# Weighing the values in three fp16 passes, with a second exp for the high halves

## What is computed

```python
h = einsum('bhid,oi,od->bho', x, weighted_sum, weight)          # x: 8, 512, 256, 4
h = h + attention(layernorm(h))                                 # 16 heads of 16, rope, q and k normed
#   scores = einsum('bhqd,bhkd->bhqk', q, k) * SCALE
#   attn = softmax(scores);  out = einsum('bhqk,bhkd->bhqd', attn, v);  out @ out_w.T + out_b
h = h + experts(layernorm(h))                                   # 8 experts, 256 -> 1024 -> 256, gated
```

## Time and profile before

| what | before |
|---|---|
| median of three runs | 2021.08 us |
| the profiled execution | 2029.17 us |
| its span, first to last instruction | 2027.4 us |
| TensorE (PE) busy | 1911.6 us, 94% |
| ScalarE (ACT) busy | 1142.6 us, 56% |
| VectorE (DVE) busy | 792.3 us, 39% |
| GpSimd (POOL) busy | 678.6 us, 33% |
| exps (line 636) | 512 of 512 columns, 262.3 + 18.0 us |
| weighing matmuls (line 788) | 1024 records, 137.2 us |

### The profile page before, as it was taken

The page is one execution under the profiler, slowest core; times in us unless marked ns, Lnnn a source line. Parts: engine busy times, 40 slices in busy tenths (PEclk is TensorE's granted clock), DMA queues, the critical chain, the costliest instruction groups (busy, mean ns, idle before and its releaser), DMA issues.

```text
span 2027.4 us, 36619 instructions
## 1 busy us (share of the span) xinstructions
PE 1911.6 (94%) x13152; PEld 1211.9 (60%) x13152; DVE 792.3 (39%) x1660; ACT 1142.6 (56%) x1969; POOL 678.6 (33%) x570
## 2 busy tenths in 40 slices
PE   5679888899999999999999999999999999999999
PEld 4246543577547764567646675467655776456666
DVE  6756933547203380145602472133810456013000
ACT  2644666544765457644765447654576446754444
POOL 1103422324323242333423343232423334233443
PEclk8779999999999999999999999999999999999999
DMA  4113332332112221131212312122221322113221
GB/s 154 38 53 113 105 130 84 123 138 84 63 64 105 97 83 63 66 130 67 84 63 87 113 66 81 63 105 95 72 75 63 109 91 84 63 63 103 104 96 53
DMA packets 40461, 176.92 MB, mean 87 GB/s; under 512 B 4056, under 2 KB 17120, under 8 KB 23904
## 3 DMA queue, kind: packets, MB, share of 16 engines
q1 hardware_dynamic: 40288, 174.52, 24.2%
HBM read 153.54 MB, written 20.97 MB: 86 GB/s over the span
## 4 chain that ended last, share of the span: by engine, by line
PE 77%; issue 7%; DVE 7%; ACT 2%; POOL 1%; ACTq 0%; DVEq 0%; POOLq 0%
PE bank_h L859 28%; PE bank_f L878 10%; PE bank_f L880 10%; PE bank_f L881 10%; PE bank_o L788 5%; PE bank_s L776 3%; PE bank_s L692 2%; PE bank_s L693 2%; PE bank_s L694 2%; DVE tmp_b L976 1%; PE bank_s L761 1%; POOL hl L549 1%; DVE y L899 1%; PE bank_s L842 1%; ACT hh L669 1%
## 5 line engine op out<-in xcount | busy, mean ns | idle before, releaser
L549 POOL TENSOR_TENSOR hl<-h,hh 128x512 f16<-128x512 f32 x512 | 608.4, 1189 | 1148.2 <-ACT hh L669 670.7
L859 PE MATMUL bank_h<-x,w1s 128*128 128x512 f16 x3072 | 756.0, 383 | 19.5 <-issue 9.1
L666 ACT ACTIVATE h<-bank_h,b1s 128x512 f32<-128x512 f32 x512 | 353.5, 690 | 468.6 <-PE bank_h L859 452.7
L878 PE MATMUL bank_f<-w2s,hh 128*128 128x256 f16 x2048 | 563.2, 275 | 2.1 <-DVE acc L1091 1.3
L880 PE MATMUL bank_f<-w2s,hh 128*128 128x256 f16 x2048 | 561.1, 274 | 0.0
L881 PE MATMUL bank_f<-w2s,hl 128*128 128x256 f16 x2048 | 560.9, 274 | 0.0
L859 PEld LDWEIGHTS bank_h<-x,w1s 128*128 128x128 f16 x3072 | 287.6, 99 | 345.7 <-issue 49.9
L669 ACT ACTIVATE hh<-bank_h,b1s 128x512 f16<-128x512 f32 x512 | 352.7, 689 | 0.0
L636 ACT ACTIVATE probs<-bank_s 128x512 f32<-128x512 f32 x480 | 262.3, 604 | 153.7 <-PE bank_s L776 153.6
L878 PEld LDWEIGHTS bank_f<-w2s,hh 128*128 128x128 f16 x2048 | 202.2, 99 | 113.8 <-issue 41.0
L1091 DVE SCALAR_TENSOR_TENSOR acc<-bank_f,gw,acc 128x256 f32<-128x256 f32 x256 | 106.1, 476 | 349.9 <-PE bank_f L881 349.8
(11 more groups left out here) (137 smaller groups left out, 1788.8 us busy)
## 6 DMA issues: line engine op xcount, KB each, us to landing
w1s<-w_parts SPq DMA_DIRECT2D x56, 1024.0 KB, 4.8
w2s<-w_parts SPq DMA_DIRECT2D x56, 1024.0 KB, 4.8
xraw<-in_x_t_dram SPq DMA_DIRECT2D x32, 512.0 KB, 4.1
raw<-in_w_dram SPq DMA_DIRECT2D x16, 1024.0 KB, 6.4
w_parts<-w1s SPq DMA_DIRECT2D x8, 1024.0 KB, 8.8
w_parts<-w2s SPq DMA_DIRECT2D x8, 1024.0 KB, 10.7
out_dram<-acc SPq DMA_DIRECT2D x16, 256.0 KB, 6.1
raw<-in_qkv_w_t_dram SPq DMA_DIRECT2D x1, 768.0 KB, 6.8
```

The lines of the kernel that those rows point to most:

```text
L549: pool.tensor_tensor(hl[n % HBUFS][:], h32[n % 2][:], hh[n % HBUFS][:], ALU.subtract)\
L666: act.activation(h32[n % 2][:], bank_h[n % 2][:, :], ACT.Relu, bias=b1s[:, e, m:m + 1]).then_inc(h_hi.sem, 1)
L859: last = pe.matmul(bank_h[n % 2][:, :], w[:, wp, k, m * P:(m + 1) * P], x16[:, xp, k, :], start=(k == 0 and wp + xp == 0), stop=(k == DK - ...
L878: pe.matmul(o, high, w[:, 0, m, :], start=(m == 0 and t % 2 == 0), stop=False, skip_group_check=True)
```

## The change

From the second batch on, the values are weighed in fp16 halves:

- The scores of two heads lie in one pair of banks (`both_s`, `both_h`), and an exp reads both at once: 1024 columns. ScalarE makes it twice, once in fp32 into `exps` (which is the memory of `qk`), once straight into fp16, the high halves. TensorE waits for both exps before it writes the next scores.
- A new VectorE step, `halves`, takes the difference of the two as the low halves, 1024 columns, 32 times a batch. It has a place of its own in the list, 0.8 of a step after its `scores`.
- `weigh` is three passes of four fp16 matmuls, in place of four fp32 matmuls. It waits for `halves`.
- The values are cut in two by VectorE: a sum into `tmp_b`, a copy to fp16, a difference, where there was one sum.
- Two exps of 512 columns for a step in the first batch stay, with the fp32 weighing; its values lie in the memory of `w2s[1]`.
- So that the values fit fp16, `projections` now begins with `scale_values`: VectorE takes a maximum over the value weights, GpSimd the maximum over the partitions, VectorE makes a power of two from it in a chain of small steps and scales the weights and the bias of the values and the output weights. ScalarE waits for that before it copies the weights.

```diff
@@ attention_order
-        steps.append((first + PACE * n, "scores", n))
+        steps += [(first + PACE * n, "scores", n), (first + PACE * (n + 0.8), "halves", n)]
@@ ScalarE, scores
+                    wait(act, scored, ab, 2 * n + 2)
+                    wait(act, qk_unit, ab, TT)
+                    wait(act, halved, ab - 1, n - 1)
+                    act.activation(exps[n % 2], score_banks(n, fb is None)[:, :, :], ACT.Exp, scale=SCORE_SCALE)\
+                       .then_inc(exped.sem, 1)
                     if half == 0:
                         wait(act, weighed, ab, u - 1)
-                    for j in range(2):
-                        wait(act, scored, ab, 2 * n + j + 1)
-                        act.activation(probs[u % 2][:, 2 * half + j, :], score_bank(2 * n + j, fb is None)[:, :], ACT.Exp,
-                                       scale=SCORE_SCALE).then_inc(exped.sem, 1)
+                    act.activation(halves[u % 2][:, 0, 2 * half:2 * half + 2, :], score_banks(n, fb is None)[:, :, :],
+                                   ACT.Exp, scale=SCORE_SCALE).then_inc(exped.sem, 1)
@@ TensorE, scores and weigh
+                    if not first_batch(fb):
+                        wait(pe, exped, ab, 2 * n)
...
+                        wait(pe, halved, ab - 1, 2 * (n + 1))
...
+                    for vp, pp in ((0, 0), (1, 0), (0, 1)):
+                        for j in range(4):
+                            h = 4 * g + j
+                            last = pe.matmul(bank_o[32 * j:32 * j + 32, :],
+                                             v1[:, vp, tile, h, :, :].rearrange("p s d -> p (s d)"),
+                                             halves[n % 2][:, pp, j, :], start=(tile == 0 and vp + pp == 0),
+                                             stop=(tile == TT - 1 and pp == 1), skip_group_check=True)
@@ VectorE, qkv and halves
+                    values = tmp_b[:, 0:D]
+                    wait(dve, summed, ab, n)
+                    half_v.link(dve, dve.tensor_tensor(values, at_v[:, 0:D], qkvb[:, 2 * D:QKV], ALU.add))
+                    values = values.rearrange("p (h d) -> p h d", d=HD)
+                    half_v.link(dve, dve.tensor_copy(v1[:, 0, n, :, 0, :], values))
+                    dve.tensor_tensor(v1[:, 1, n, :, 0, :], values, v1[:, 0, n, :, 0, :], ALU.subtract)\
                        .then_inc(qkv_out.sem, 1)
...
+                elif stage == "halves":
+                    u, half = divmod(n, 2)
+                    high, low = (halves[u % 2][:, part, 2 * half:2 * half + 2, :] for part in range(2))
+                    wait(dve, exped, ab, 2 * n + 2)
+                    dve.tensor_tensor(low, exps[n % 2], high, ALU.subtract).then_inc(halved.sem, 1)
@@ projections
-                    act.wait_ge(proj_in, 32)
+                    act.wait_ge(v_scaled, 1)
+                elif stage == "projections":
+                    pool.wait_ge(v_max, 1)
+                    pool.partition_all_reduce(vmxr[:], vmx[:], P, bass.bass_isa.ReduceOp.max).then_inc(v_max_all, 1)
+            def scale_values():
+                dve.wait_ge(proj_in, 32)
+                dve.tensor_reduce(vmx[:], w_v, AX.X, ALU.max, apply_absolute_value=True).then_inc(v_max, 1)
...
+                dve.wait_ge(v_max_all, 1)
...
+                dve.tensor_scalar(w_v, w_v, vscl[:, 0:1], None, ALU.mult)
+                dve.tensor_scalar(raw_out, raw_out, vscl[:, 1:2], None, ALU.mult)
+                dve.tensor_scalar(b_v, b_v, vscl[:, 0:1], None, ALU.mult).then_inc(v_scaled, 1)
```

More of the change, by code:

```diff
@@ L143, in bodies @@
     first = [("mix_weights", 0)]
-    for step in attention_order(alone=True):
+    for step in [s for s in attention_order(alone=True) if s[1] != "halves"]:
         first += [step[1:]] + between.get(step[1:], [])
@@ L208, in bank, with two_banks @@
             return ctx.enter_context(nc.psum_tensor(name, [P, 512], F32))
+        def two_banks(name):
+            return ctx.enter_context(nc.psum_tensor(name, [P, 2, 512], F32))
         def sem(name):
@@ L251, in build @@
         kt = sb("kt", [P, HEADS // 2, TOKENS], F16)
-        v1 = sb("v1", [P, TT, HEADS, 2, HD])
+        v1 = sb("v1", [P, 2, TT, HEADS, 2, HD], F16)
+        v_first = w2s[1][:].rearrange("p s k d -> p (s k d)").bitcast(F32)\
+            .rearrange("p (t h s d) -> p t h s d", t=TT, h=HEADS, s=2)
         probs = [sb(f"probs{i}", [P, 4, TOKENS]) for i in range(2)]
+        halves = [p[:].rearrange("p j t -> p (j t)").bitcast(F16).rearrange("p (s j t) -> p s j t", s=2, j=4)
+                  for p in probs]
+        exps = [qk[:, 2 * i:2 * i + 2, :] for i in range(2)]
         xh = sb("xh", [P, XK, P], F32R)
@@ L292, in build @@
         scl = sb("scl", [P, 2])
-        bank_s = [bank(f"bank_s{i}") for i in range(2)]
+        vmx = sb("vmx", [P, DK])
+        vmxr = sb("vmxr", [P, DK])
+        vbound = sb("vbound", [P, 2])
+        vscl = sb("vscl", [P, 2])
+        both_s = two_banks("bank_s")
+        bank_s = [both_s[:, i, :] for i in range(2)]
         bank_m = bank("bank_m")
         bank_o = bank("bank_o")
-        bank_h = [bank(f"bank_h{i}") for i in range(2)]
+        both_h = two_banks("bank_h")
+        bank_h = [both_h[:, i, :] for i in range(2)]
         bank_f = [bank(f"bank_f{i}") for i in range(2)]
@@ L308, in build @@
         mix_made = [sem(f"mix_made{i}") for i in range(2)]
+        v_max = sem("v_max")
+        v_max_all = sem("v_max_all")
+        v_scaled = sem("v_scaled")
         set_hi = sem("set_hi")
@@ L379, in build, with score_banks, first_batch @@
         block = ctx.enter_context(nc.Block())
-        def score_bank(n, alone):
-            return ([bank_s[0], bank_s[1], bank_h[0], bank_h[1]] if alone else bank_s)[n % (4 if alone else 2)]
+        def score_banks(n, alone):
+            return both_h if alone and n % 2 else both_s
+        def first_batch(fb):
+            return fb is None
         def qkv_banks(t, alone):
@@ L673, in steps @@
                     act.wait_ge(scales, e + 1)
+                    if e == 1 and p == PIECES // 2:
+                        wait(act, weighed, 0, UNITS)
                     if e >= 2 and p == 0:
@@ L779, in steps @@
                     g, tile = divmod(n, TT)
-                    wait(pe, exped, ab, 4 * (n + 1))
+                    if first_batch(fb):
+                        wait(pe, exped, ab, 4 * (n + 1))
+                    else:
+                        wait(pe, halved, ab - 1, 2 * (n + 1))
                     if n == 0:
@@ L785, in steps @@
                         wait(pe, o_out, ab, g)
-                    for j in range(4):
-                        h = 4 * g + j
-                        last = pe.matmul(bank_o[32 * j:32 * j + 32, :],
-                                         v1[:, tile, h, :, :].rearrange("p s d -> p (s d)"),
-                                         probs[n % 2][:, j, :], start=(tile == 0), stop=(tile == TT - 1),
-                                         skip_group_check=True)
+                    if first_batch(fb):
+                        for j in range(4):
+                            last = pe.matmul(bank_o[32 * j:32 * j + 32, :],
+                                             v_first[:, tile, 4 * g + j, :, :].rearrange("p s d -> p (s d)"),
+                                             probs[n % 2][:, j, :], start=(tile == 0), stop=(tile == TT - 1),
+                                             skip_group_check=True)
+                        last.then_inc(weighed.sem, 1)
+                        return
+                    for vp, pp in ((0, 0), (1, 0), (0, 1)):
+                        for j in range(4):
+                            h = 4 * g + j
+                            last = pe.matmul(bank_o[32 * j:32 * j + 32, :],
+                                             v1[:, vp, tile, h, :, :].rearrange("p s d -> p (s d)"),
+                                             halves[n % 2][:, pp, j, :], start=(tile == 0 and vp + pp == 0),
+                                             stop=(tile == TT - 1 and pp == 1), skip_group_check=True)
                     last.then_inc(weighed.sem, 1)
@@ L917, in steps @@
                         att_v.start(ab)
+                        if not first_batch(fb):
+                            half_v.start(ab - 1)
                     wait(dve, x_in[n % 2], ab, 16 * (n // 2 + 1))
```

45 lines of the change are left out of this document (39 added, 6 removed).

## The result

The changed kernel takes 2168.14 us (median of four, 2166.88 to 2169.57), against 2024.07 for the kernel before, run beside it (four, 2020.14 to 2027.73): 1.071 times as long, 95% interval 1.069 to 1.073. The forecast was 2120, with 2060 to 2190 as its range. The profiled executions stand 137.7 us apart in their spans (2027.4 and 2165.1), where the sum had 99.

A forecast was written before the change was run, and what follows sets the result against it. TensorE alone was taken to set the pace in the score steps. Merged batches 72, second batch 18, values' steps 1 and start 8 made +99 us on 2029.2, or 2128; from the median 2021, 2120. Range 2060 to 2190.

The forecast's parts named there:

- The exp: ScalarE's exp of 1024 columns: 0.90 us from one to the next, two holding ScalarE 1.80 in place of 0.98.
- The weighing: Three fp16 passes on TensorE: 0.80 us in place of 1.00, bounds 0.77 and 0.96; 0.6 gained a round.
- The walk of a round: Six score steps: TensorE waits 1.49, 0.68 and 0.41 us for exps; 18.14 in place of 16.16.
- The front of a batch: Values' two more VectorE steps ahead of the rotation, about 0.4 us each: 1 us for all 28 tiles, bounds 0 and 25.
- The second batch: Score steps beside the experts' preparation, with ScalarE late: +18 us, bounds 6 and 26; VectorE's halves put at 0.
- The start: Scaling delays ScalarE's weight copies, v_scaled at 24.5 us: +8, bounds 4 and 11; extra memsets fall into GpSimd's waiting.
- TensorE wasn't the bound: Rival, chance 0.07: TensorE stays the bound in the score steps, a round is 15.56 us, 2007 in all.
- ScalarE wasn't full either: Rival, chance 0.09: ScalarE is the bound with hand-overs hidden, 15.8 us a round, 2023 in all.
- the three passes do run side by side: Rival, chance 0.03, claimed they don't: a weighing takes 2.76 us, a round 21.4, 2227 in all.
- the rival on the clock: Chance 0.10: after TensorE's waits in the rounds the clock falls to 1.2 GHz, 67 us on top, 2187.

## Why the prediction was right, and by how much it was short

The direction and the mechanism were right, and the time lies in the range, 48 us above the number. 39 of these are missing in the sum, by the two profiled executions; the rest is the spread of the kernel before (2020 to 2028), from whose low end the forecast started. Step by step:

- **The exp**: 0.90 from one to the next and 1.04 long, as taken from the copy of 1024 columns. The Trainium skill (ScalarE: Activation LUTs, Rules for kernel authors) has about 0.3 us and 0.83 ns an element for an instruction with its bias as a pointer operand. The estimate of 1.15 from it doesn't apply here, since the exps have no such operand, and the rows of this case held.
- **The weighing**: 0.77, where 0.80 was taken; that is the low bound, so nothing of the dozen weight loads shows.
- **The walk of a round**: waits of 1.49, 0.68 and 0.41 were predicted, 1.40 to 1.66, 0.74 and 0.41 measured, at the very scores named, and 94.3 us for the steps (18.25 a round) where 18.14 a round and 94 were forecast. The run without the large fp32 exp shows that the second exp is the cause, the one with the old order that the order is worth 2.7 us of the 12, and those with high halves from VectorE (81.0) and of high exps alone (76.3) that nothing else in the change holds the steps up by more than the 1.2 us of waits for VectorE in the former.
- **The front of a batch** was mis-sized: 1 us was taken for the values' steps in all, and batch 3 shows 2.0 a batch. The run with one step gives back 0.9 of it; the other 1.1 stays open, though the two waits of which the 2.0 are made do go with the values' steps. The cast among them takes 1.26 us, where about 0.4 was taken: see below. With it, a batch costs 13.4 in place of 12.2, +7 over six.
- **The second batch**: 15.5 where 18 was taken, 14.0 of them in its score steps (120.0 us against 106.0). The prediction named ScalarE as the cause and put VectorE at 0. TensorE's waits there are 16.5 us for ScalarE and 18.2 us for VectorE's low halves, since VectorE also cuts the experts' weights, so 0 isn't shown to hold. But these 18.2 us aren't VectorE's price either: before, TensorE waited 13.3 us for exps in the same steps. With the small fp32 exp the weighing still waits 15.1 us for VectorE, and the steps take 104.7 us, less than before:

```profile
PE bank_o L843 <- DVE probs L1077: 15.1, 7, 4.0
```

  That points to the second exp for most of the 14.0. As that kernel also shortens VectorE's step, no run parts the two. That VectorE can hold up this batch the kernel with its extra copies shows (118.8 us for the steps, with no second exp at all).
- **The start**: 9.6 where 8 was taken. The maximum over the partitions began 5.70 us after GpSimd had got free, near the 5.98 of the earlier trace rows, and took 0.37; but GpSimd had got free 1.6 later than the forecast had it. The two extra memsets aren't the reason: they lie in its waiting, as forecast, of which 1.71 us are left, and the cast is released by the landing of `b2sb` at 16.6 us. It lands at 15.6 to 16.8 us in all other kernels, those with the memsets of before included; the trace of the kernel before, with 14.73, was the early one. ScalarE began its copies at 25.38 against 16.47. In the changed kernel:

```profile
16.60 0.29 POOL L603 CAST ident<-ident 128x128 f16<-128x128 f32 x1 [1.71 <-DMA b2sb<-in_b_dram]
...
22.59 0.37 POOL L585 PARTITION_ALL_REDUCE vmxr<-vmx  x1 [5.70 <-issue]
...
25.38 1.48 ACT L609 ACTIVATE qkvw<-raw 128x1536 fp32r<-128x1536 f32 x1 [7.96 <-DVE qkvb L1209]
```

- **What was missing**: the stop at the loop top and the lower clock behind it, 6 to 8 us in each of five batches, 32 us of the 39 that the sum is short. No term of the prediction asked where the code of TensorE comes to lie. That it counts is shown both ways: the kernel before gets the stop by 128 instructions more ahead of the loop, and the changed one loses it by another 128. That gives back 30 of the 32 us; the stops alone are 24.4.
- **The rivals**: TensorE wasn't the bound, ScalarE wasn't full either, the clock stayed at its upper level in the steps, and the three passes do run side by side. The clock did fall elsewhere, in the fronts, behind a stop that the rival on the clock didn't have in view.

The sum again, with what was measured: 9.6 (start) + 15.5 (second batch) + 6 x 13.4 (a batch) + 32 (loop top) = 137.5 us, against 137.7. The 32 are what the other terms leave, so this sum had to close; the check on them is the 30 us of the run that takes the stop away.

## What to carry to other kernels

Before an operation is doubled on the engine with time to spare, look at the buffer between the two engines: with one pair of banks the round is the sum of making, reading and handing back, and an engine at 71% can set the time before it is full. A step that costs nothing in one stage has to be costed again in every stage in which its engine has other work. And when a change adds or removes instructions, look for a stop with no releaser behind the loop top in both traces, ahead of any theory of the operations themselves: it can be as large as the effect that is looked for, and the clock can fall behind it.

## What was not expected of the hardware

**The place of the loop's code.** The shift of TensorE's code ahead of the loop, against the kernel before, counted over all of TensorE's instructions in the traces up to the first `f1` of the loop, how much longer the loop itself is, and whether the stop after seven matmuls is there:

| kernel | shift ahead of the loop | loop | stop |
|---|---|---|---|
| before; high halves only, with and without scaling | 0 | 0 | none |
| changed; small exp; old order; values in one step; no scaling | +128 | +99 | 3.3 to 5.1 us |
| high halves on VectorE | +128 | +130 | 4.7 to 5.2 us |
| before with turns twice, in the loop too | +128 | +128 | 3.2 to 5.2 us |
| before with turns twice once | +128 | 0 | 4.7 to 5.1 us |
| one pass | -128 | -157 | 4.2 to 4.8 us |
| changed with turns twice once | +256 | +99 | none |

0 and 256 are free of it, 128 either way is not, and the length of the loop itself makes no difference to whether it comes. Instructions arrive by a DMA queue of their own. In the changed kernel, around the loop top of 1476.42 us (a window of 30 us):

```profile
q8 instruction: 4, 0.07, 0.9%
```

Four packets of some 16 KB each. One lands about 3 us after the hand-over of `x` and the next some 7 us behind it, in the kernel before as well; whether TensorE runs dry in between depends, by this reading, on how much of the first piece lies behind the loop's top. The stop ends with the second landing: in all 45 stops of the nine kernels that have them, TensorE goes on 1.2 to 1.5 us after it, as it starts the pass 1.7 to 1.9 us after the first. The Trainium skill states such a mechanism (Runtime: NRT & Kernel Launch, Instruction fetch mechanics): code comes in blocks of 16 KiB, 256 instructions, one after the other, and a branch to a block that isn't at hand waits until it is fetched. The table and the packets agree: 256 instructions more leave all as it was. A shift other than a multiple of 128 was not tried. What stays open is why the second block comes so late, and no run here was made for that.

**VectorE and GpSimd beside each other.** The values' cast of 256 columns takes 1.26 us on average, though a copy of 2048 fp16 columns at the hand-over takes 0.68. In the trace it ends 0.15 us behind GpSimd's product, all 28 times:

```profile
499.30 1.27 POOL L579 TENSOR_TENSOR tmp_a<-qk,cos 128x512 f32<-128x512 f32 x1 [2.08 <-DVE qk L1021]
499.43 1.29 DVE L1031 CAST v<-tmp_b 128x256 f16<-128x256 f32 x1
...
1476.42 0.68 DVE L1140 COPY x<-x16n 128x2048 f16<-128x2048 f16 x1
```

In the kernel with the high halves made on VectorE, GpSimd's difference (1.22 us on average in the changed kernel) takes 2.23 us in places (up to 3.20 in the changed kernel as well):

```profile
578.92 2.23 POOL L572 TENSOR_TENSOR hl<-h,hh 128x512 f16<-128x512 f32 x1 [3.59 <-ACT hh L705]
```

The traces hold the comparison. In the changed kernel GpSimd's difference takes 1.18 us at most in the 242 cases in which VectorE does nothing beside it, and 1.93 on average in the 18 beside the low halves of line 1077 alone. In the kernel with the copies, VectorE's cast of 1024 columns takes 0.68 to 0.70 us without GpSimd (116 cases) and up to 1.66 beside its difference. So with each of these two pairs the long durations go with the overlap, though no run was made that takes it away alone. It isn't so for every pair: GpSimd's product takes 1.27 us with the values' cast beside it and 1.27 in the kernel without that cast. For the cast itself, which never stands alone, it isn't shown.
